# Identity and first low parts moved to VectorE, the passage between two stages prepared in the last channels, ScalarE issuing the first stacks, four mixing banks

## The chip, the cores and the metric

The kernel runs on one core of one Trainium2 chip. The core has five engines: TensorE (matmuls, into PSUM), VectorE, ScalarE, GpSimd, and SyncE, which here only issues DMAs; ScalarE and GpSimd can issue DMAs too. In the profile they are PE (PEld for TensorE's weight loads), DVE, ACT, POOL and SP. The metric is the device time of one execution, in microseconds.

## The reference

The input x has 128 samples, 64 channels and 1024 times, float32. Four steps follow one another, each adding to x:

```python
x = x + _L0_cond_ref(x, itok_B_8_3872, log_dt, C, log_A_real, A_imag, D)   # y = causal conv of (x*mask) along time
                                                                           #     with one kernel per channel, + D*x, * mask
x = x + _L1_cond_ref(x, itok_B_0_15, weights)       # einsum('bct,bcd->bdt', x, weights[condition]): 64x64 mixing of channels
x = x + _L2_cond_ref(x, itok_B_6_15, W2, bias, A2, B2)   # x @ W2.T + bias + (x @ A2[id].T) @ B2[id].T, rank 16
x = x + _L3_cond_ref(x, itok_B_0_2, W3, A3, B3)          # x @ W3.T + 0.5 * (x @ A3[id]) @ B3.T, rank 32
```

The mask is `arange(1024) < length` of each sample (step L0); the convolution kernel K of a channel is 2 Re sum_n Cs exp(dtA l) over 64 states. W2 and W3 are 1024 x 1024.

## The kernel before, in words

Products in float32 are replaced by three passes with two-part operands: each operand is split into a high part (a copy rounded to the type fp32r, made by ScalarE) and a low part (original minus high part, made by VectorE or GpSimd), and `PASSES` takes high x high, high x low and low x high.

**First block, preparation.** Since the L2 and L3 steps follow each other, their weights are merged into one matrix, (I + W2')(I + W3'). SP loads the eight 512 KB row blocks of W3 (`w3_raw`) and of W2 (`p2`). For each W3 block i an engine adds the identity to the block's diagonal part (`w3_identity`), ScalarE makes the high part `p3[:, i, 0]` and VectorE the low part (`p3_low`). The W2 blocks get an identity (`p2_identity`) and are staged in two buffers: `stage_high(n)` on ScalarE, `stage_low(n)` on GpSimd. TensorE runs 24 jobs in the order of the list `ORDER`, each into one of four PSUM targets of 1024 columns: d0, d4, the parameters of the convolution (`par`), the adapter products a3a and a3b, b2_0 to b2_2, c, row, b3, k0 and k1 (which build the convolution kernels from factors fac_u and fac_v), la0 to la3, d1, d5, d2, d6, d3, d7, b2_3. A job waits until the user before it of its target was read (`job_free`). d0 waits for `p3_lo` of each block in turn and for `staged_lo`. Meanwhile VectorE computes exponentials and the states' factors in a long chain of small operations on 64 x 64 elements, where every one waits for the one before (`link`): `exp_parts` first on `logs`, then on `decay`, up to `base_ready`; then the bias products, then the readers of the jobs. GpSimd makes the constants, the identities, the low parts and four large products of factors (128 x 2048), in this order: fac_v, fac_t, two times fac_u, fac_v, stage_low(4), fac_t.

**First block, convolution.** 64 channels, in groups of 8 (`UNROLL`), channel u of a group in buffer u % 4 for loads and u % 2 for the rest. Each channel's samples (`xt`) are multiplied with a Toeplitz table made from `lags`; 5.76 us of TensorE a channel. ScalarE makes high parts (`split_high`) for the next channel and copies the front half out (`front`), VectorE makes the low parts (`split_low`) and the back half (`back`). SP loads three channels ahead and stores each channel (`store_y`) to x1_d in HBM. After the last channel SP waits until its last stores have landed; this ends the block, and all engines go to the second block together.

**Second block.** 64 tiles of 128 rows (two samples of 64 channels) in 32 pairs. Each tile's x1 is loaded (`x1_in`), and for times past the sample's length `choose` puts the original x (`x_nat`) in its place: VectorE makes two 256-column pieces of a mask `late`, then a predicated copy of 512 columns. Four mixing quarters (`quarter`, 128 x 512 each, by the gathered mixing matrix `m_gath`) go through one PSUM bank, `MIX_BANK`; `take` on ScalarE copies each out, once as it is and, for three of them, as a high part. The pair's two tiles are multiplied with the merged 1024 x 1024 matrix by a scheme of seven products of quadrants (M1 to M7, Strassen-Winograd), with operands a11, s1, a12, a22, s2, s4, s3. The adapters' 96 columns (`h_table`, written by `h_high` and `h_low` from `tab2` and `tab3`, of which the second tile's is first made a `difference`) ride in M1, M5, M2 and M4; their results go through a small adapter product (`c_gath`, `hc`) into `hs`, and `low_rank` multiplies them with `stack`. In `pair(n)` of every engine's program the work of pair n+1 is prepared within pair n; only the first pair's preparation stands ahead of the loop, between the blocks. There, SP loads x1, x and the first tile's tables, ScalarE issues the second's, then SP loads `c_gath` and the stacks; GpSimd clears `m_gath` and fills `c_gath` before it gathers; VectorE chooses, sets fixed parts of `hrow`, `hc`, `hs` (twelve small instructions with `fix`), then makes the low parts.

Of the kernel before, what the change touches and what calls it, by code (L numbers as in the profile page):

```python
# [12 lines left out]
P = 128  # L13
# [30 lines left out]
def program(nc, x, xt_in, steps, cond, adapter, labeler, log_dt, ssm_c, log_a_real, a_imag, ssm_d,  # L44
# [143 lines left out]
    for i in range(1, 3):  # L188
        lags[i], o = at(f"lags{i}", [P, T], F32, o)
# [3 lines left out]
    b2_last, _ = at("b2_last", [P, 2, T], F32R, o)  # L193
# [21 lines left out]
    stack = both("stack", [P, 2, T], F32R)  # L215
    x1_in = both("x1_in", [P, T])
    x_nat = both("x_nat", [P, T])
    late = place("late", [P, HB], U16)
    tab2 = both("tab2", [P, 2, K8, R2])
    tab3 = both("tab3", [P, 2, K8, R3])  # L220
    m_gath, c_gath = both("m_gath", [P, P]), both("c_gath", [P, P])
    hrow, hc, hs = both("hrow", [P, P]), both("hc", [P, P]), both("hs", [P, 2, P], F32R)
# [55 lines left out]
    w3_ready, p2_ready = sem("w3_ready"), sem("p2_ready")  # L278
# [32 lines left out]
    b2_rows = b2_d.rearrange("a r h t -> (a r) h t")  # L311

    with nc.Block() as block:
        @block.sync
        def _(sp):
# [85 lines left out]
            for u in range(UNROLL):  # L401
                channel(GROUPS - 1, u, loads=False)
            for u in range(2):
                sp.wait_ge(x1_stored[u], count_in(GROUPS, 0, 2))
            sp.wait_ge(b2_stored, 16 * (AR // P))
# [3 lines left out]
            sp.wait_ge(a3_stored, 16)  # L409

        @block.gpsimd
        def _(pool):
# [43 lines left out]
            def w3_identity(i):  # L456
                pool.wait_ge(in_w3[i], 16)
                block_of = w3_raw[:, i, i * P:(i + 1) * P]
                tt(block_of, block_of, ident[:], ALU.add).then_inc(w3_ready, 1)

# [49 lines left out]
        def _(act):  # L510
# [12 lines left out]
            def stage_high(n):  # L523
# [4 lines left out]
                elif name[0] == "b":  # L528
                    act.wait_ge(in_b2, 16)
                else:  # L530
                    act.wait_ge(p2_ready, (1, 2, 0, 0, 0, 3, 4, 5, 6, 9, 10)[n])
# [26 lines left out]
            for i in range(K8):  # L558
# [4 lines left out]
                if i == K8 - 2:  # L563
                    act.wait_ge(trig_in, 1)
# [1078 lines left out]
```

## Time and profile before

| | us |
|---|---|
| median of 3 timed runs | 1518.61 (1517.77 to 1518.9) |
| the profiled execution | 1514.85 |
| its span, first to last instruction | 1512.9 |
| TensorE busy | 1458.1 (96%) |
| VectorE busy | 1118.1 (74%) |
| ScalarE busy | 630.9 (42%) |
| GpSimd busy | 134.9 (9%) |

A busy share is a mean over the stages: up to about 130 us the preparation runs, then the last preparation jobs and the convolution until 577.7 us, then the paired stage. "Idle before, <-X" at a row means that the engine stood for so long until X released it.

### The profile page before, as it was taken

The numbers are of one execution on the slowest core, as the hardware profiler recorded it, in microseconds if no ns is written. First come the engines' busy times: TensorE is split into PE (matmuls) and PEld (weight loads), VectorE is DVE, ScalarE is ACT, GpSimd is POOL, SyncE is SP. The second block draws the span as 40 slices with busy tenths as digits, with TensorE's granted clock in tenths as the row PEclk, the third lists the DMA queues.
The fourth block names the chain that finished last, engine by engine and source line by source line (L and its number), as shares of the span: only waits on it lengthen the run. The fifth ranks groups of instructions, "written<-read, shape, count | busy, mean of one in ns | idle before, by whom it ended". The sixth has DMA issues, their size and how long they took to land.

```text
span 1512.9 us, 33953 instructions
## 1 busy us (share of the span) xinstructions
PE 1458.1 (96%) x10624; PEld 1405.8 (93%) x10624; DVE 1118.1 (74%) x2320; ACT 630.9 (42%) x1249; POOL 134.9 (9%) x198
## 2 busy tenths in 40 slices
PE   6979999999999996999999999999999999999998
PEld 4867889999999995999999999999999999999998
DVE  7874478888888885677777777777777777777774
ACT  3330256566665652334334334334334334334332
POOL 6460210000000000000000000000000000000000
PEclk9989999999999996999999999999999999999999
DMA  8034068888888775445645645645655645645652
GB/s 303 17 134 114 11 205 286 276 274 270 275 275 271 276 248 182 160 147 162 193 146 162 193 146 162 193 146 160 195 146 159 195 146 158 197 146 156 198 146 78
DMA packets 121235, 276.15 MB, mean 183 GB/s; under 512 B 23881, under 2 KB 64333, under 8 KB 118545
## 3 DMA queue, kind: packets, MB, share of 16 engines
q1 hardware_dynamic: 110988, 241.67, 52.3%
q10 hardware_dynamic: 10214, 34.06, 5.6%
q8 instruction: 18, 0.29, 0.1%
q14 instruction: 15, 0.12, 0.0%
HBM read 200.72 MB, written 74.95 MB: 182 GB/s over the span
## 4 chain that ended last, share of the span: by engine, by line
PE 59%; DMA 1%; DVE 0%; issue 0%; ACT 0%; DVEq 0%; ACTq 0%; SPq 0%
PE ps L1537 23%; PE ps L1538 23%; PE ps L1508 8%; PE ps L1545 2%; PE ps L1547 2%; PE ps L1519 1%; DMA out<-y_out 1%; PE ps L1514 0%; DMA x_nat<-in_x 0%; ACT a L1282 0%; DVE weights L1399 0%; ACT xa L1284 0%; ACT weights L1294 0%; DVE x_in L1373 0%; DVE y_out L1486 0%
## 5 line engine op out<-in xcount | busy, mean ns | idle before, releaser
L1537 PE MATMUL ps<-weights,xs 128*128 128x256 f32 x1536 | 396.1, 289 | 0.0
L1538 PE MATMUL ps<-weights,xs 128*128 128x256 f32 (+1 forms) x1536 | 387.3, 291 | 0.0
L1537 PE MATMUL ps<-weights,xa 128*128 128x352 f32 (+1 forms) x1152 | 328.9, 314 | 4.6 <-DVE weights L1399 1.3
L1538 PE MATMUL ps<-weights,xa 128*128 128x256 f32 (+1 forms) x1152 | 322.8, 295 | 0.0
L1538 PEld LDWEIGHTS ps<-weights,xs 128*128 128x128 f32 x1536 | 292.3, 190 | 0.0
L1537 PEld LDWEIGHTS ps<-weights,xs 128*128 128x128 f32 x1536 | 291.3, 190 | 0.0
L1068 PE MATMUL ps<-toep,ut 128*128 128x512 f32 (+2 forms) x1152 | 228.2, 343 | 0.0
L1537 PEld LDWEIGHTS ps<-weights,xa 128*128 128x128 f32 x1152 | 216.9, 188 | 10.1 <-issue 10.1
L1538 PEld LDWEIGHTS ps<-weights,xa 128*128 128x128 f32 x1152 | 217.9, 189 | 0.0
L1068 PEld LDWEIGHTS ps<-toep,ut 128*128 128x128 f32 x1152 | 195.5, 190 | 16.8
L1282 ACT ACTIVATE a<-ps 128x512 f32<-128x512 f32 x128 | 76.7, 599 | 282.4 <-PE ps L1508 281.9
L1508 PE MATMUL ps<-m_gath,x_in 128*128 128x128 f32 x1024 | 139.1, 280 | 13.8 <-DVE x_in L1373 10.4
L1508 PEld LDWEIGHTS ps<-m_gath,x_in 128*128 128x128 f32 x1024 | 128.1, 196 | 14.8 <-DVE x_in L1373 12.2
L1256 POOL COPY m_gath<-mix 64x64 f32 x128 | 50.7, 396 | 826.1 <-PE ps L1508 713.7
L971 PE MATMUL ps<-p,staged 128*128 128x512 f32 x480 | 111.7, 394 | 12.6 <-POOL staged L454 10.4
L971 PEld LDWEIGHTS ps<-p,staged 128*128 128x128 f32 x480 | 91.2, 191 | 32.5 <-issue 10.8
L619 ACT ACTIVATE ut<-xt 128x896 fp32r<-128x896 f32 x64 | 61.0, 953 | 137.4 <-PE ps L1079 131.6
L1373 DVE COPY_PREDICATED x_in<-late,x_nat 128x512 f32<-128x512 uint16 x128 | 95.7, 747 | 19.5 <-DVE late L1368 19.5
L1079 PE MATMUL ps<-toep,ut 128*128 128x256 f32 x768 | 107.3, 289 | 0.0
L1079 PEld LDWEIGHTS ps<-toep,ut 128*128 128x128 f32 x768 | 95.8, 190 | 0.0
L903 DVE TENSOR_TENSOR ut<-xt,ut 128x896 fp32r<-128x896 f32 x64 | 69.9, 1093 | 16.7 <-ACT ut L619 16.7
L1294 ACT ACTIVATE weights<-tab 128x128 fp32r<-128x128 f32 (+1 forms) x256 | 71.3, 352 | 25.2 <-DVE tab L1390 25.2
(218 smaller groups left out, 2194.6 us busy)
## 6 DMA issues: line engine op xcount, KB each, us to landing
lags<-kern_d SPq DMA_DIRECT2D x64, 512.0 KB, 5.1
xt<-in_xt SPq DMA_DIRECT2D x64, 512.0 KB, 5.8
x_d<-yo SPq DMA_DIRECT2D x64, 512.0 KB, 2.9
x_in<-x_d SPq DMA_DIRECT2D x64, 512.0 KB, 5.9
x_nat<-in_x SPq DMA_DIRECT2D x64, 512.0 KB, 3.9
out<-y_out ACTq DMA_DIRECT2D x64, 512.0 KB, 5.5
stack<-b_d SPq DMA_DIRECT2D x130, 128.0 KB, 3.6
tab<-a_d SPq DMA_DIRECT2D x126, 128.0 KB, 2.1
```

The source lines that it names most:

```text
L619: copy(ut[u % 2][:, 0, 0:SPLIT], xt[u % BUFS][:, 0:SPLIT], ACT.Copy).then_inc(ut_hi, 1)
L903: tt(ut[u % 2][:, 1, 0:SPLIT], xt[u % BUFS][:, 0:SPLIT], f(ut[u % 2][:, 0, 0:SPLIT]), ALU.subtract).then_inc(ut_lo, 1)
L971: ins = mm(t[:, cols], staged[n % 2][:, a, c, :], p3[:, c, b, cols], start=c == a == b == 0, stop=c == K8 - 1 and a == 1)
L1068: mm(y[:, half * HB + i * P:(half + 1) * HB], xs[:, a, half * half_t + i, :], tp[:, b, 0:HB - i * P], start=i == a == b == 0, stop=False)
L1079: ins = mm(y[:, to:to + QT], xs[:, a, i, :], tp[:, b, at_col:at_col + QT], start=False, stop=i == half_t - 1 and a == 1)
L1256: ins = nc.gpsimd.tensor_copy(m_gath[v][rows, b * C:(b + 1) * C], mix[rows, bass.ds(s, 1), :].squeeze(1))
L1282: ins = copy(raw[:], mixing, ACT.Copy)
L1294: ins = copy(to, of, ACT.Copy)
L1373: nc.vector.copy_predicated(x1_in[v][:, cols], late[:], x_nat[v][:, cols]).then_inc(chosen[v], 1)
L1508: ins = mm(acc[:, MIX_BANK, i * P:(i + 1) * P], x1_in[v][:, c * P:(c + 1) * P], m_gath[v][:], start=True, stop=True)
L1537: mm(left[0], x_part, left[1], start=first and is_wide, stop=end, skip_group_check=True)
L1538: ins = mm(right[0], x_part, right[1], start=first and is_wide and H_AT[m] > 0, stop=end, skip_group_check=True)
```

## The change: what it does

- **Head.** The identity of W3's blocks and of p2[0], and the low part of the first staged block, move from GpSimd to VectorE, into a function `triangle` that runs within the first `exp_parts`, after the step with 1/720; the p3 low parts move in with them. ScalarE's two sine tables come after `stage_high(1)`. On GpSimd stage_low(4) moves ahead of the second fac_v product. A new semaphore `p2_first` counts p2[0].
- **Last channels.** SP loads the first pair's adapter tables after the loads of the last channels and the store of channel 60, and x of the first two tiles ahead of the store of channel 62; it issues the loads of x1 as soon as the stores have landed, still in the first block. ScalarE runs `h_high` of the first pair ahead of the last channel's `front`; VectorE runs `difference`, the masks of the first pair (eight, in `late_first`) and `h_low` around the last `back`. The SBUF tiles of the second block are placed so that these lie in buffers that are free by then.
- **Second block, first pair.** The quarters go into four banks without waiting for one another's reads; VectorE chooses in the order of the quarters, with no masks to make; its fixes come after `sums(0)`. GpSimd gathers before it fills `c_gath`. ScalarE issues the first stack loads; SP the rest.
- **Last pair.** VectorE makes y21 before y22, and the last tile's store is issued in two halves.

```diff
+            def triangle():
+                dve.wait_ge(consts, 2)
+                w3_identity(0)
+                dve.wait_ge(in_w2[0], 16)
+                tt(p2[0][:, 0, :], p2[0][:, 0, :], ident[:], ALU.add).then_inc(p2_first, 1)
+                p3_low(0)
+                w3_identity(1)
+                dve.wait_ge(staged_hi, 1)
+                tt(staged[0][:, 1], p2[0][:], f(staged[0][:, 0]), ALU.subtract).then_inc(staged_lo, 1)
+                for i in range(1, K8):
+                    if i + 1 < K8:
+                        w3_identity(i + 1)
+                    p3_low(i)
...
-            for i in range(K8):
-                w3_identity(i)
-                if i == 0:
-                    p2_identity(p2[0], 0, in_w2[0])
-                    stage_low(0)
             for i in BLOCKS[1:]:
                 p2_identity(p2[i], i, in_w2[i])
                 if i == 1:
+                    pool.wait_ge(staged_lo, 1)
                     stage_low(1)
...
+            stage_low(4)
             pool.wait_ge(fac_arg, 2)
             tt(fac_v[:], across(1), steps_of(1), ALU.mult).then_inc(fac_turns, 1)
-            stage_low(4)
...
# SP, end of the first block
-            for u in range(UNROLL):
+            for u in range(UNROLL - 3):
                 channel(GROUPS - 1, u, loads=False)
...
+            sp.wait_ge(toep_lo, C - 2)
+            sp.wait_ge(tri_ready, C - 2)
+            for v in range(2):
+                load_tables(sp, v, ids(sp, 0, v, B), ids(sp, 0, v, 2 * B))
+            channel(GROUPS - 1, UNROLL - 3, loads=False)
+            sp.wait_ge(toep_lo, C - 1)
+            sp.wait_ge(tri_ready, C - 1)
+            sp.wait_ge(conv_done, C - 3)
+            for v in range(2):
+                sp.dma_start(x_nat[v][:], x_rows[v]).then_inc(x_landed[v], 16)
+            channel(GROUPS - 1, UNROLL - 2, loads=False)
+            channel(GROUPS - 1, UNROLL - 1, loads=False)
+            for u in range(2):
+                sp.wait_ge(x1_stored[u], count_in(GROUPS, 0, 2))
+            for v in range(2):
+                sp.dma_start(x1_in[v][:], x1_rows[v]).then_inc(x1_landed[v], 16)
...
# ScalarE, last group of channels
             for u in range(UNROLL):
+                if u == UNROLL - 1:
+                    for v in range(2):
+                        h_high(act, 0, v)
                 channel(GROUPS - 1, u, ahead=u < UNROLL - 1)
...
# VectorE, last group of channels
-            for u in range(UNROLL):
+            for u in range(UNROLL - 1):
                 channel(GROUPS - 1, u, ahead=UNROLL - 1 - u)
+            difference(dve, 0)
+            dve.wait_ge(conv_done, C - 1)
+            for v in range(2):
+                for q in range(4):
+                    nc.vector.tensor_scalar(late_first[:, 2 * v + q // 2, q % 2 * QT:q % 2 * QT + QT], ramp[:], float(q * QT),
+                                            lens_cols[:, v:v + 1], ALU.add, ALU.is_ge).then_inc(masked, 1)
+            h_low(dve, 0, 0)
+            back(GROUPS - 1, UNROLL - 1)
+            h_low(dve, 0, 1)
...
# second block, ScalarE
-            load_tables(act, 1, ids(act, 0, 1, B), ids(act, 0, 1, 2 * B))
-            take(0, 0, a11, xa11)
-            take(0, 1, a21)
-            take(0, 2, a22, xa22)
-            h_high(0, 0)
+            for v in range(2):
+                load_stack(act, v, ids(act, 0, v, B))
+            take(0, 0, a11, xa11, FIRST_BANKS[0])
+            take(0, 1, a21, None, FIRST_BANKS[1])
+            take(0, 2, a22, xa22, FIRST_BANKS[2])
             s1_high(0)
-            h_high(0, 1)
-            take(0, 3, a12, xa12)
+            take(0, 3, a12, xa12, FIRST_BANKS[3])
...
# second block, TensorE
-            def quarter(n, q):
+            def quarter(n, q, bank=MIX_BANK):
...
-                ready(pe, quarter_read, 4 * n + q)
+                if bank == MIX_BANK:
+                    ready(pe, quarter_read, 4 * n + q)
...
+                if last_one:
+                    act.dma_start(out_rows[2 * n + 1, :, 0:HB], y_out[1][:, 0:HB]).then_inc(y_stored[1], 16)
+                    act.wait_ge(y22_added, n + 1)
+                    act.dma_start(out_rows[2 * n + 1, :, HB:T], y_out[1][:, HB:T]).then_inc(y_stored[1], 16)
```

`FIRST_BANKS = (MIX_BANK, SMALL_BANK, V_OWN, S_OWN)`; M1 writes to two others.

## Rows read from the trace of the kernel before

**Rows 1.** The page: span, and busy time (share of span) xinstructions by engine.

```profile
span 1512.9 us, 33953 instructions
PE 1458.1 (96%) x10624; PEld 1405.8 (93%) x10624; DVE 1118.1 (74%) x2320; ACT 630.9 (42%) x1249; POOL 134.9 (9%) x198
```

**Rows 2.** TensorE's waits: who waited for whom, us in total, times, longest.

```profile
PE ps L1059 <- DVE dt L909: 3.5, 2, 2.5
```

**Rows 3.** Timeline, 0 to 60 us: start, us, engine, line, operation, xcount, idle before.

```profile
8.69 0.49 POOL L463 TENSOR_TENSOR p<-p,ident 128x128 f32<-128x128 f32 x1 [0.92 <-DMA p<-in_L_cond_base_weight]
...
10.34 2.38 POOL L454 TENSOR_TENSOR staged<-p,staged 128x1024 fp32r<-128x1024 f32 x1 [1.17 <-ACT staged L534]
...
14.81 13.67 PE L980 MATMUL ps<-p,staged 128*128 128x512 f32 x48 [14.81 <-DVE p L668]
...
25.12 2.38 DVE L672 TENSOR_SCALAR e_k<-n 64x64 f32<-64x64 f32 x1
...
43.84 0.75 DVE L748 TENSOR_SCALAR b3t<-w_raw,bias_col 128x1024 f32<-128x1024 f32 x1
...
48.55 0.42 DVE L760 COPY part<-ps 128x256 f32<-128x256 f32 x1 [2.64 <-PE ps L995]
```

**Rows 4.** Tile w_raw, 0 to 30 us: xcount, ns min/median/max, first and last start.

```profile
L668 DVE TENSOR_TENSOR p<-w_raw,p x8: 1206/1226/1485, 13.6 to 24.0; 128x1024 fp32r<-128x1024 f32 x8
```

**Rows 5.** Timeline, 56 to 175 us, the jobs b2_0 to d1.

```profile
58.91 22.06 PE L971 MATMUL ps<-p,staged 128*128 128x512 f32 x96 [1.58 <-DVE raw L776]
...
86.82 4.39 POOL L454 TENSOR_TENSOR staged<-b2raw,staged 128x1024 fp32r<-128x1024 f32 x1
...
91.36 12.95 PE L971 MATMUL ps<-p,staged 128*128 128x512 f32 x48 [10.39 <-POOL staged L454]
...
115.31 0.66 DVE L845 COPY c_out<-ps 128x480 f32<-128x480 f32 x1 [4.47 <-PE ps L957]
...
127.53 47.69 PE L971 MATMUL ps<-p,staged 128*128 128x512 f32 x209 [0.61 <-DVE lora_out L869]
```

**Rows 6.** Timeline of SP's queue, 556 to 605 us.

```profile
561.33 17.59 SPq L371 DMA_DIRECT2D x_d<-yo  x4
581.66 0.34 SPq L1178 DMA_DIRECT2D x_in<-x_d  x1
...
583.00 0.43 SPq L1181 DMA_DIRECT2D x_nat<-in_x  x1
586.12 0.35 SPq L1167 DMA_DIRECT2D tab<-a_d  x1
```

**Rows 7.** Timeline, 556 to 605 us: ScalarE, VectorE and TensorE around the passage.

```profile
574.80 0.59 ACT L635 ACTIVATE yo<-ps 128x512 f32<-128x512 f32 x1
...
586.75 0.48 DVE L1368 TENSOR_SCALAR late<-ramp,lens_cols 128x256 uint16<-128x256 int16 x2 [8.24 <-DMA x_nat<-in_x]
...
588.17 2.08 PE L1508 MATMUL ps<-m_gath,x_in 128*128 128x128 f32 x8 [10.45 <-DVE x_in L1373]
...
592.60 0.17 DVE L1379 MEMSET hrow<- 128x128 f32 x1
...
594.95 0.69 DVE L1404 TENSOR_TENSOR xa<-a,xa 128x512 fp32r<-128x512 f32 x1
...
600.98 0.55 PE L1537 MATMUL ps<-weights,xa 128*128 128x256 f32 x1 [1.28 <-DVE weights L1399]
...
603.64 0.36 PE L1537 MATMUL ps<-weights,xa 128*128 128x256 f32 x1
```

**Rows 8.** The DMA view, issues by line: xcount, KB each, median us from issue to landing.

```profile
tab<-a_d SPq DMA_DIRECT2D x126, 128.0 KB, 2.1
...
tab<-a_d ACTq DMA_DIRECT2D x2, 128.0 KB, 5.0
```

**Rows 9.** The chain of waits, in order of time: a later quarter.

```profile
794.87 0.89 PE ps L1508 x8
```

**Rows 10.** Timeline, 1503 to 1513 us: the last issue.

```profile
1509.70 0.35 ACTq L1341 DMA_DIRECT2D out<-y_out  x1
```

More of the change, by code:

```diff
@@ new lines, in program, with over_pairs @@
+    PAIRS = TILES // 2
+    c_adapters = c_d[0:AR].rearrange("(a r) c -> a r c", r=R2)
+    x1_rows = x1_d.rearrange("(n b) c t -> n (b c) t", b=2)
+    x_rows = x.rearrange("(n b) c t -> n (b c) t", b=2)
+    out_rows = out.rearrange("(n b) c t -> n (b c) t", b=2)
+    H3 = slice(R2, R2 + R3)
+    def over_pairs(eng, body, end=PAIRS - 1):
+        body(0, False)
+        with eng.Fori(1, end) as n:
+            body(n, False)
+        for n in range(end, PAIRS):
+            body(n, n == PAIRS - 1)
@@ new lines, in halves, with load_stack @@
+    def halves(ap):
+        return ap.rearrange("p (k c) -> p k c", k=2)
+    first_rows = [sem(f"first_rows{v}") for v in range(2)]
+    masked = sem("masked")
+    def load_stack(eng, v, a):
+        for b in range(2):
+            row = b * (R2 + R3)
+            eng.dma_start(f(stack[v][row:row + R2]), b2_d[bass.ds(a[b], 1)].squeeze(0)).then_inc(stack_landed[v], 16)
+            eng.dma_start(f(stack[v][KS + row:KS + row + R2, 0]),
+                          b2_d[bass.ds(a[b], 1), :, 0, :].squeeze(0)).then_inc(stack_landed[v], 16)
@@ new lines, in h_high, with difference @@
+    def h_high(act, n, v):
+        act.wait_ge(tab_landed[v], 64 * n + 64)
+        if v == 1:
+            act.wait_ge(diffed, 2 * n + 2)
+        for m, part_of in products_of(v):
+            for to, of in zip(h_table(0, m), tables(v, part_of)):
+                ins = nc.scalar.activation(to, of, ACT.Copy)
+        ins.then_inc(h_hi[v], 1)
+    def difference(dve, n):
+        dve.wait_ge(tab_landed[1], 64 * n + 64)
+        for t in (tab2[1], tab3[1]):
+            nc.vector.tensor_tensor(t[:, :, K4:K8], t[:, :, K4:K8], t[:, :, 0:K4], ALU.subtract).then_inc(diffed, 1)
@@ L313, in program, with h_low @@
+    def h_low(dve, n, v):
+        dve.wait_ge(h_hi[v], n + 1)
+        if v == 1:
+            dve.wait_ge(diffed, 2 * n + 2)
+        for m, part_of in products_of(v):
+            for to, high, of in zip(h_table(1, m), h_table(0, m), tables(v, part_of)):
+                ins = nc.vector.tensor_tensor(to, of, f(high), ALU.subtract)
+        ins.then_inc(h_lo[v], 1)
     with nc.Block() as block:
@@ L679, in exp_parts @@
                     link(stt(q, q, 1.0 / n, r, ALU.add, ALU.mult))
+                    if n == 720 and between is not None:
+                        between()
                 link(ts(ki, k, 127.0, None, ALU.add))
@@ L694, in _ @@
             tt(frac[:], turns[:], tmp[:], ALU.subtract).then_inc(trig_in, 1)
-            for i in range(K8):
-                p3_low(i)
             exp_parts(decay[:], e_k[:, 0:N], e_f[:, 0:N], e_q[:, 0:N], e_2k[:, 0:N], e_i[:, 0:N])
@@ L1128, in program @@
-    PAIRS = TILES // 2
-    c_adapters = c_d[0:AR].rearrange("(a r) c -> a r c", r=R2)
-    x1_rows = x1_d.rearrange("(n b) c t -> n (b c) t", b=2)
-    x_rows = x.rearrange("(n b) c t -> n (b c) t", b=2)
-    out_rows = out.rearrange("(n b) c t -> n (b c) t", b=2)
-    H3 = slice(R2, R2 + R3)
-    def over_pairs(eng, body, end=PAIRS - 1):
-        body(0, False)
-        with eng.Fori(1, end) as n:
-            body(n, False)
-        for n in range(end, PAIRS):
-            body(n, n == PAIRS - 1)
@@ L1285, in take @@
                 ins.then_inc(quarter_read, 1)
-            def h_high(n, v):
-                act.wait_ge(tab_landed[v], 64 * n + 64)
-                if v == 1:
-                    act.wait_ge(diffed, 2 * n + 2)
-                for m, part_of in products_of(v):
-                    for to, of in zip(h_table(0, m), tables(v, part_of)):
-                        ins = copy(to, of, ACT.Copy)
-                ins.then_inc(h_hi[v], 1)
             def s1_high(n):
```

264 lines of the change are left out of this document (131 added, 133 removed).

## The prediction

> **What bounds the kernel now.** I read the busy line of the page first. TensorE is busy 1458.1 of the 1512.9 us span, so only some 55 us of TensorE's absence can be won anywhere [rows 1]. Next the list of TensorE's waits: behind three entries of over 10 us the next is 3.5 us [rows 2]. In all there are three large holes. One is the start: no matmul before 14.81 us, which waits for VectorE's low part of the first W block [rows 3]. One is inside the preparation: 10.4 us before the job b2_2 at 91.36, which waits for GpSimd's low part [rows 5]. One is the passage from the convolution to the paired stage: four mixing quarters of 2.05 us each spread from 588.17 to 600.98, after 10.45 us without a matmul, and then matmuls that stay long until 603.64: a record of L1537 is 0.55 us at 600.98 and 0.36 there, the first of the short ones [rows 7]. The paired stage itself (31 more pairs) has no hole worth naming. So the change can act in those three places and at the last store; the steady loops are the same code.
>
> **The start: identity and first low parts on VectorE.** After the change VectorE interrupts its exp chain after eight small operations, at about 7.5 us. p2[0] is on chip at 8.69 (GpSimd's add starts then) [rows 3], its identity is added by 9.0. One p3_low takes 1.21 us at best and 1.49 at worst [rows 4], so p3_low(0) ends at 10.2; the identity of block 1 (a 128x128 add; I take 0.3 us, GpSimd needs 0.49 for one [rows 3]) at 10.5; the low part of p2[0], same size as p3_low, at 11.8. GpSimd's version of that step took 2.38 us and began at 10.34 [rows 3]. The first matmul moves from 14.81 to about 11.8.
>
> That does not go to the end by itself, because VectorE's chain, not TensorE, sets when the next hole closes. Seven more rounds of 1.22 + 0.3 us, and 0.6 for meeting GpSimd, end the triangle near 23. Then GpSimd's second low part blocks VectorE: before, an operation of 0.2 us at 25.12 took 2.38 beside it [rows 3]. I let VectorE go on at 25.4. Fourteen small links of the interrupted chain are left, 0.28 us each (the pitch from 25.12 to 43.84, less its three stalls [rows 3]): 29.3, and 0.5 for GpSimd's remaining adds: 29.8. From there to the bias products the old chain took 43.84 - 25.12 = 18.7 us; 2.2 of stall and 0.8 of slowed links now lie ahead of it, so 15.7: the bias products begin at 45.5, 1.7 later than before. Two of them take 2.05; TensorE, early enough by then, has its transposed parameters at 46.0, so the copy that was at 48.55, behind a wait, comes at 47.6. The chain behind it (six bias products, the first lower_low) is 1.0 us earlier, and b2_0 starts near 57.9 instead of 58.91 [rows 3, 5]. Of the 3 us won at the first matmul, 2 turn into a wait for the parameters and before b2_0. Bounds: with every p3_low at 1.49 and each identity as slow as GpSimd's 0.49, b2_0 is 2 us later than that; if GpSimd's adds never meet it, 1 earlier.
>
> On that hangs one place where the Trainium skill speaks against the edit. The worst p3_low is 0.28 us above the best, and the small operation beside GpSimd's low part took 2.38 instead of 0.2 us [rows 3, 4]. The page "SBUF — State Buffer" (section "Who interferes with whom") says that a VectorE instruction with two SBUF inputs contends with a GpSimd instruction that reads SBUF, and whichever issues first holds the port for the whole instruction. By the rule the seven adds that GpSimd keeps would all hold up VectorE, 7 x 0.49 = 3.4 us instead of my 0.6, and the time would be 2.8 us above my forecast; by the row at most 8 x 0.28 = 2.2 us, 1.6 above it.
>
> **stage_low(4) ahead of the third factor product.** TensorE ends b2_1 at 58.91 + 22.06 = 80.97, now 79.9 [rows 5]. GpSimd ends its second fac_u product at 81.2 (where the next one began), now 80.1; the low part, which had stood behind a product of 5.7 us, starts at once and takes 4.39 as before (VectorE still holds it up; alone 2.38 [rows 3, 5]). b2_2 starts at 84.5 instead of 91.36. The factor product comes later by the same 4.4 us, but its reader on VectorE was not ready before about 89 anyway, and the two products together take what they took; the factors are 1 us earlier, as everything here. What is late next is VectorE again: from 104 us on it runs low parts, c, row, b3, the split constants, kern and lora copies one behind another until d1 may start at 127.53. Its idle time for TensorE in that chain was 4.47 us before the copy of c, and 0.35 after it [rows 5]. TensorE now brings c some 7 us earlier, so these 4.8 vanish, and no more; the store of the third b2 block then comes 0.3 us after VectorE wants it. So d1 starts 1.0 + 4.8 - 0.3 = 5.5 us earlier, and from there TensorE is continuous. Bounds of the whole head: 2.0 (VectorE's chain 3.5 later) and 7.5 (b2_0 a microsecond earlier still, and a low part of 2.38).
>
> **Work moved into the last channels.** SP issues the store of channel 60 at 561.33 [rows 6]. Behind it now come eight ids and eight table loads. Four ids cost it 2.7 us (from the end of its issue at 583.00 to 586.12), four table loads 1.9, so it is busy 9.2 us, until about 570.9, and the store of channel 61 is issued there instead of at 567.1. ScalarE needs that buffer again at 574.8 [rows 7]; the store lands 2.9 us after issue: 573.8, one us of cover. The x_nat loads follow, then the store of 62 on time. The last table lands 2.1 us after issue (the SP row; the ScalarE rows, behind 2 MB of loads, say 5.0) [rows 8], at 573.0. VectorE then does the differences (0.6), eight masks of 0.24 [rows 7] (1.9) and four lows (1.2): 576.8, under the end of the last channel at 577.7. ScalarE's highs end near 575. All of this is free, with 0.9 us of cover on VectorE. With a landing of 5.0 the last back part would be 2.2 late; that is the bound.
>
> **The passage.** The first instruction of the second block came at 581.66, when the last store had landed; x_nat[0], queued behind x1, was there at 586.75, 5.1 later [rows 6, 7]. Now x1 alone is loaded, issued by SP at 581.5 ahead of the block's end. A 512 KB load alone I put at 4.0 us, between the last store's 2.9 and that 5.1: landed 585.5. The masks are made, so one predicated copy (0.73) follows: first quarter at 586.4, 1.8 earlier than 588.17. GpSimd's gathers now come ahead of its c_gath work, the second done by 586.5, just in time. With four banks no quarter waits for ScalarE. Two quarters at the low clock (2.05 each) and two at the high one (0.89 each [rows 9]) end at 592.4, since b2_2 after its hole lost 12.95 - 22.06/2 = 1.9 us, so about 3.8 us pass at the low level of 1.2 GHz [rows 5]. ScalarE issues the stack loads first (four ids, eight DMAs at 0.5: to 589.2) and takes quarter 0 by 590.3; the low part is there at 591.1, and the tables are long split. So M1 starts at 592.4 instead of 600.98: 8.6. M1 runs at the high level at once: it had lost (603.64 - 600.98)/2 = 1.3. Together 9.9.
>
> Some is given back. M5 ends 6.5 us after M1 starts, at 598.9. M2 wants the copy of the first product out of PSUM, and ScalarE's queue has it behind s4's high part, which waits for VectorE's s4. VectorE now has its twelve fixes (592.60 to 594.95, 2.35 us [rows 7]) between the sums and the pair: sums end 594.7, fixes 597.1, s2, a12's low and s4 (0.65 each) 599.0, ScalarE's two copies of 0.6 [rows 7] 600.25. TensorE stands 1.35 us before M2. Net 8.5. Bounds 5 (x1 at 5.9, tables at 5.0) and 10.5 (no wait at M2, x1 at 3.3).
>
> **The last store.** Its issue is at 1509.70 and the span ends 3.2 us later [rows 10]. Halved, it moves 256 KB last instead of 512; at most 0.6, I take 0.2.
>
> **Sum.** 5.5 + 8.5 + 0.2 = 14.2 us. The profiled execution took 1514.85 us (span 1512.9 and 1.9 around it); it was 3.8 us faster than the median 1518.61 of the timed runs. I take the difference off the median: 1504.4.
>
> **Rivals.**
> A: VectorE in the head is blocked more than I allow, b2_0 starts later than before, the head brings 2. For it: the 2.38 for a 0.2 us operation. Against it: GpSimd has little to do until 17 us. 1507.9.
> B: SP's table block comes too late and the last back part waits 2.2 us. For it: 0.9 us of cover only. 1506.6.
> C: the clock stays at the low level through all four quarters and into M1 (before it did so through four spaced ones). 2.3 + 1.3 lost: 1508.0.
> D: no wait at M2, because x1 or ScalarE is quicker: 1503.
> E, the slower side: the low level lasts through pair 0 of the second stage, because short waits (M2's above all) keep breaking TensorE's work there. A pair is about 28 us of work at the high level, which would take twice that: 1504.4 + 28 + 1.3, about 1534. From 28 us of clock time at the low level on (14.2 us lost) the change is no gain. Against it: before, the clock rose 2.7 us into M1 and stayed [rows 7].
>
> **Chances.** Forecast 0.46, A 0.15, B 0.10, C 0.12, D 0.09, E 0.04, and 0.04 that A, B and C meet and leave nothing to be seen. A measurement here can tell about 0.2% (3 us) from no change: faster 0.92, same 0.04, slower 0.04. The range is 1499.5 to 1510.5: from both best bounds to A and C together.
>
> **What would show it.** First matmul near 11.8; a wait for the parameters near 45; b2_0 near 57.9 and b2_2 near 84.5; d1 near 122; the last channel's end with no new wait before its store; 8.7 us from the last convolution matmul to the first quarter; four quarters back to back in some 6 us, M1 6 us after the first quarter; a wait of 1 to 2 us before M2. I am wrong if b2_2 moves and d1 does not, if the last channel's back part waits for VectorE, or if M1 comes later than 595 (in the old times).

## The result, and the profile after

Median of 4 timed runs 1503.74 us (1502.53 to 1505.15), against 1518.19 (1517.1 to 1518.9, 4 runs) of the kernel before on the same chip: ratio 0.9908, 95% interval 0.9893 to 0.9922, 14.45 us less. The forecast was 1504.4. The profiled execution took 1502.63 us, its span is 1500.9 ([rows 1]: 1512.9).

The busy line of the page, to be read against [rows 1]:

```profile
PE 1456.2 (97%) x10624; PEld 1404.1 (94%) x10624; DVE 1114.5 (74%) x2330; ACT 631.1 (42%) x1249; POOL 117.3 (8%) x188
```

TensorE's matmuls are the same 10624. Its time without a matmul went from 54.8 to 44.7 us: that is 10.1 of the 12.0 us, and the other 1.9 are busy time. Its waits (who waited for whom, us in total, times, longest):

```profile
PE ps L1145 <- DVE staged L821: 11.8, 1, 11.8
PE ps L1573 <- DVE x_in L1455: 8.9, 1, 8.9
PE ps L1136 <- POOL staged L595: 4.8, 1, 4.8
PE ps L1225 <- DVE dt L1065: 4.6, 3, 2.4
PE ps L1209 <- DVE kern L1018: 2.8, 1, 2.8
...
PE ps L1602 <- ACT y_out L1386: 1.3, 2, 1.1
```

All three large holes are shorter, and the waits of the later quarters (2.5 and 0.8 before) are gone. The wait behind the copy of `kern` grew from 0.7 to 2.8 us, the one for `dt` in the convolution from 3.5 to 4.6. The last entry is new: it holds the wait before M2 (1.1).

**The head.** Timeline of all engines, 5 to 60 us (start, us, engine, line, operation, xcount, idle before), against [rows 3]:

```profile
10.26 0.29 DVE L806 TENSOR_TENSOR w_raw<-w_raw,ident 128x128 f32<-128x128 f32 x1
10.47 1.22 DVE L821 TENSOR_TENSOR staged<-p,staged 128x1024 fp32r<-128x1024 f32 x1
11.60 0.29 DVE L806 TENSOR_TENSOR w_raw<-w_raw,ident 128x128 f32<-128x128 f32 x1
11.83 13.97 PE L1145 MATMUL ps<-p,staged 128*128 128x512 f32 x48 [11.83 <-DVE staged L821]
...
18.49 2.62 DVE L810 TENSOR_TENSOR p<-w_raw,p 128x1024 fp32r<-128x1024 f32 x2
19.41 0.62 POOL L599 TENSOR_TENSOR p<-p,ident 128x128 f32<-128x128 f32 x1 [14.31 <-DMA p<-in_L_cond_base_weight]
...
20.61 0.82 POOL L599 TENSOR_TENSOR p<-p,ident 128x128 f32<-128x128 f32 x1 [0.58 <-DMA p<-in_L_cond_base_weight]
21.04 4.09 DVE L836 SCALAR_TENSOR_TENSOR e_q<-e_q,e_f 64x65 f32<-64x65 f32 x5
21.39 2.39 POOL L595 TENSOR_TENSOR staged<-p,staged 128x1024 fp32r<-128x1024 f32 x1
...
43.72 0.75 DVE L904 TENSOR_SCALAR b3t<-w_raw,bias_col 128x1024 f32<-128x1024 f32 x1
...
45.88 0.42 DVE L916 COPY part<-ps 128x256 f32<-128x256 f32 x1
```

The first matmul is 3.0 us earlier, and VectorE reaches the bias products at 43.72, as early as before (43.84). TensorE's timeline of the jobs b2_0, b2_2, the lora transposes and d1, against [rows 5]:

```profile
56.24 22.05 PE L1136 MATMUL ps<-p,staged 128*128 128x512 f32 x96 [1.57 <-DVE raw L932]
83.05 12.56 PE L1136 MATMUL ps<-p,staged 128*128 128x512 f32 x48 [4.76 <-POOL staged L595]
...
118.09 2.22 PE L1209 MATMUL ps<-ident,lora_a_raw 128*128 128x128 f32 x16 [2.76 <-DVE kern L1018]
120.91 19.33 PE L1136 MATMUL ps<-p,staged 128*128 128x512 f32 x84 [0.60 <-DVE lora_out L1025]
```

b2_0 is 2.7 us earlier, b2_2 8.3, d1 6.6. The 1.7 lost between are on VectorE's timeline, 92 to 122 us:

```profile
107.31 0.65 DVE L1001 COPY c_out<-ps 128x480 f32<-128x480 f32 x1
...
112.90 1.40 DVE L1011 CAST b_out<-b3t 1x1024 fp32r<-1x1024 f32 x2 [1.86 <-DMA b_d<-b_out]
...
116.82 2.34 DVE L1018 COPY kern<-ps 32x1024 f32<-32x1024 f32 x2
```

The wait of 4.47 before the copy of c is gone; the split constants wait 1.86 for the store that leaves their buffer free, and `kern`, queued behind them, is what TensorE waits for.

**The passage.** Timeline of SP's queue, VectorE and TensorE, 549 to 603 us, against [rows 6, 7]:

```profile
564.48 0.37 SPq L499 DMA_DIRECT2D x_d<-yo  x1
...
566.18 0.63 DVE L429 TENSOR_TENSOR tab<-tab 128x128 f32<-128x128 f32 x2 [0.28 <-DMA tab<-a_d]
...
570.90 0.42 DVE L1073 TENSOR_TENSOR yo<-ps,shared_in 128x256 f32<-128x256 f32 x1 [1.45 <-PE ps L1245]
575.36 0.82 SPq L550 DMA_DIRECT2D x_in<-x_d  x2
...
578.96 0.73 DVE L1455 COPY_PREDICATED x_in<-late_first,x_nat 128x512 f32<-128x512 uint16 x1 [6.23 <-DMA x_in<-x_d]
...
579.74 6.21 PE L1573 MATMUL ps<-m_gath,x_in 128*128 128x128 f32 x32 [8.88 <-DVE x_in L1455]
```

The last back part (570.90) waits for TensorE, not for the tables: all moved work is under cover. In the trace the store of the last channel lands 3.57 us after its issue at 571.73; in the trace before it was 2.61. In front of it SP has put 1 MB of x_nat, issued at 564.95, of which the second half lands at 572.76, and the store of channel 62, issued at 566.25, which lands at 574.08 (7.8 us later; 2.6 before). So the early x_nat loads are probably not free: the stores issued behind them land later than before, and x1 isn't loaded until the last store has landed. No run here has x_nat at another place, so this stays unproven. The wait before the first quarter is 8.88 instead of 10.45, and the 32 matmuls of the four quarters are one group without idle time. The same stretches of both kernels by engine (stretch, us, busy time and (x) of PE, PEld, DVE, ACT, POOL, then PEclk, DMA share, GB/s): hole, quarters, M1 and M5 until M2. Before:

```profile
577.72:588.17 10.45, 0.00 (x1) 0.00 (x1) 1.97 (x5) 0.00 (x0) 2.05 (x10) 0.60 0.62 236
588.17:600.98 12.81, 8.22 (x33) 7.16 (x33) 9.77 (x30) 6.24 (x16) 0.43 (x1) 0.50 0.71 172
600.98:608.92 7.94, 7.94 (x49) 7.94 (x49) 6.36 (x14) 2.42 (x5) 1.22 (x3) 0.82 0.94 312
```

After:

```profile
570.86:579.74 8.88, 0.00 (x1) 0.00 (x1) 2.56 (x7) 0.00 (x0) 0.98 (x5) 0.69 0.72 274
579.74:585.71 5.97, 5.97 (x32) 5.76 (x33) 2.64 (x4) 2.19 (x5) 1.05 (x6) 0.61 0.94 173
585.71:593.81 8.10, 6.96 (x51) 6.74 (x50) 6.92 (x19) 3.96 (x8) 0.94 (x4) 1.00 0.94 262
```

TensorE works through all of the quarters' stretch (5.97 of 5.97 us; before 8.22 of 12.81), and the granted clock is 1.00, the 2.4 GHz level, from M1 on; before it was still low there (0.82). From M1 to M2, though, 8.10 us pass with only 6.96 of work: M2 waits for ScalarE's copy (1.14). From the last convolution matmul to M2 it is 22.95 instead of 31.20 us: 8.25 less. With the 6.86 by which the convolution ends earlier, M2 comes 15.1 us earlier (608.92, 593.81).

At the end of the span only 12.0 are left. Between lie the pairs of the paired stage. From the start of M1 in the second pair to its start in the last, 30 pairs, it is 852.5 us in the profile before and 855.2 after: 2.8 given back before rounding. Before, 29 of the 30 are 28.4 us long. After, 11 are, and 16 are 28.53 or 28.54, without a longer wait of TensorE; these make some 2.1 of it, in code that the change doesn't touch. The rest lies in single longer pairs, the third above all (28.94). The last store is issued 3.3 us before the end of the span, against 3.2 [rows 10]: nothing from the halves.

### The profile page after: what moved, and what is told of

It is laid out like the page before. It is cut to its first block, busy times and chain, and to the rows that moved or that the text cites. A ratio compares the mean times of both kernels' runs of the same rounds, so it can differ in the third digit from the quotient of the medians.

```text
span 1500.9 us, 33974 instructions
## 1 busy us (share of the span) xinstructions
PE 1456.2 (97%) x10624; PEld 1404.1 (94%) x10624; DVE 1114.5 (74%) x2330; ACT 631.1 (42%) x1249; POOL 117.3 (8%) x188
## 4 chain that ended last, share of the span: by engine, by line
PE 87%; DVE 6%; DMA 3%; POOL 1%; issue 1%; ACT 1%; SPq 0%; DVEq 0%; ACTq 0%; POOLq 0%
PE ps L1602 23%; PE ps L1603 23%; PE ps L1234 13%; PE ps L1573 8%; PE ps L1245 6%; PE ps L1136 4%; PE ps L1225 3%; PE ps L1610 2%; PE ps L1612 2%; PE ps L1237 2%; DMA out<-y_out 1%; PE ps L1584 1%; DVE p L810 1%; DVE b3t L906 1%; DMA b_d<-b_last 1%
## 5 line engine op out<-in xcount | busy, mean ns | idle before, releaser
L1334 POOL COPY m_gath<-mix 64x64 f32 x128 | 46.1, 360 | 823.0 <-PE ps L1573 719.9
L1447 DVE COPY_PREDICATED x_in<-late,x_nat 128x512 f32<-128x512 uint16 x124 | 92.5, 746 | 18.9 <-DVE late L1442 18.9
L422 ACT ACTIVATE weights<-tab 128x128 fp32r<-128x128 f32 (+1 forms) x256 | 71.4, 353 | 26.6 <-DVE tab L429 26.5
```

Of the source, the lines that this page charges most:

```text
L422: ins = nc.scalar.activation(to, of, ACT.Copy)
L1334: ins = nc.gpsimd.tensor_copy(m_gath[v][rows, b * C:(b + 1) * C], mix[rows, bass.ds(s, 1), :].squeeze(1))
L1447: nc.vector.copy_predicated(x1_in[v][:, cols], late[:], x_nat[v][:, cols]).then_inc(chosen[v], 1)
```

## The experiments

Each ratio is against the kernel before, on the same chip. Where no ratio stands, the kernel ran once, and its time says little about a few us, since the runs of one kernel lie 1 to 6 us apart; such a run is read from its milestones. Milestones are from the profile of each. "Conv end" is the end of the last convolution matmul, q0 the first mixing quarter.

### The two halves of the change, each alone

Before, with the head's edits only:

```diff
+            def triangle(): ...            # identity, p3 low parts, stage_low(0) on VectorE
+            stage_low(4)                   # GpSimd, ahead of the second fac_v product
             tt(fac_v[:], across(1), steps_of(1), ALU.mult).then_inc(fac_turns, 1)
-            stage_low(4)
```

> The kernel before with the head's edits alone (triangle on VectorE, stage_low(4) ahead of the second fac_v product, sine tables later); second block and SBUF layout as before. Theory: the head is worth what the changed kernel's trace shows, d1 starting near 120.9 instead of 127.53, and passes on to the end unshortened: 6.6 us, a time near 1511.6, first convolution matmul 6.7 earlier, passage unchanged (10.4 us of wait, quarters spread over 12.8). Rival: the convolution's start waits for something else (its tables, the last low parts), and under 3 us arrive. On the paired stage: if its 28.53 us pairs in the changed kernel come from the new placement of the second block's tiles, all pairs are 28.40 here; if they are a matter of the run, some here are 28.5 too.

Measured: 1512.1 against 1519.41 us, ratio 0.9958 (0.9941 to 0.9974), 7.3 less. First matmul 11.9, b2_0 56.3, b2_2 83.1, d1 121.33; the passage is no shorter than before: q0 10.33 after conv end (10.45 before), M2 21.8 after q0 (20.8). The head's share of the gain is the head's edits alone.

The whole change without those:

```diff
-            def triangle(): ...
-            stage_low(4)                   # back behind the fac_v product, identities back on GpSimd
```

> The changed kernel with the head as it was before: the passage, the four banks, the layout and the last pair's edits alone. Theory: the passage is worth 8.4 us up to M2 of the first pair and the last store 0.2, independent of the head: near 1509.6 if the longer pairs are a matter of the run, near 1512.4 if the new placement causes them (then pairs of 28.5 us here). Sum of this gain and that of the head alone within 1.5 us of the changed kernel's. Rival: head and passage overlap in what they win (one shared limit), then the sum of the two single gains is over 17 us.

Measured: 1511.52 against 1519.41, ratio 0.9952 (0.9935 to 0.9968), 7.9 less. q0 8.46 after conv end, M1 6.1 after q0, M2 14.2 after q0 with a wait of 1.29. The halves don't need each other.

The changed kernel once more beside both:

> The changed kernel again, unedited. If the 28.53 us pairs come from its layout, most pairs have them again (25 to 60 percent at 28.39 were seen); if they are a matter of the run, the share changes widely, to none or to all. Time 1502.5 to 1505.2.

Measured: 1506.91 against 1519.41, ratio 0.9916 (0.9899 to 0.9932), 12.5 less, and outside the range expected; the halves' sum is 15.2. Each of the three differences is known to some 2.5 us, so 12.5 and 15.2 may well be the same. In these profiles 5 of 30 pairs are 28.53 us long with the head alone, 2 with the passage alone, and 27 with the whole change (857.5 us in all, 5.0 over the profile before). Of the 5.0, 27 times 0.13 are 3.5; another 1.3 is the third pair alone, of 29.66 us, in which TensorE waits 1.0 for ScalarE's copy out of PSUM. With the old passage (the kernel before, and the head alone) the second and third pairs are 28.40 to 28.53; with the new one, one of the two is 28.6 to 29.7 in every run. So a part of what the paired stage gives back follows the change; what holds ScalarE up there was not traced further.

Is it the code's layout that makes the pairs longer? The changed kernel a third time, on another chip:

> The changed kernel once more, on the same chip as the combined version, for the difference of the two and for the spread of three things between executions: landing of the last store (3.6 and 4.9 us seen), share of 28.53 us pairs, time at the low clock after the passage.

Measured: 1503.71 against 1517.14, ratio 0.9912 (0.9896 to 0.9929), 13.4 less; here 25 of the 30 pairs are 28.4 (853.9 us). Groups by line and shape, 610 to 1450 us (count, busy us, mean ns, idle before), first of the second run, then of this one:

```profile
L1603 PE MATMUL ps<-weights,xa 128*128 128x352 f32 x360 | 102.1, 325 | 0.0
L1603 PE MATMUL ps<-weights,xs 128*128 128x352 f32 x349 | 99.0, 326 | 0.0
```

```profile
L1603 PE MATMUL ps<-weights,xa 128*128 128x352 f32 x360 | 100.5, 320 | 0.0
L1603 PE MATMUL ps<-weights,xs 128*128 128x352 f32 x360 | 99.7, 317 | 0.0
```

The same program has both lengths, so layout alone doesn't decide it; the matmuls of 352 columns in M1 and M5 are longer, without a wait. What decides between them stays open.

### Four banks or one

```diff
-    FIRST_BANKS = (MIX_BANK, SMALL_BANK, V_OWN, S_OWN)
+    FIRST_BANKS = (MIX_BANK,) * 4
```

> The changed kernel with the four first quarters in one bank again, each waiting for the read of the one before. Theory: before, the quarters were 2.8 to 3.5 us apart; with the choices made early the pace is quarter plus ScalarE's copies (2.05 + 1.1 or 0.6, and s1's high part before the fourth), and the clock stays low: M1 starts about 6 us later than 585.7 (after the first quarter: 12 instead of 6), M1 at the low clock another 1.3; the wait of 1.1 before M2 disappears, since VectorE has the time. Net 5 to 6 us worse. Rival: the early tables and masks alone bring the quarters together and the banks are worth under 2 us.

Measured, one run: 1511.9 against 1519.41; the changed kernel on the same chip took 1506.91. TensorE's timeline:

```profile
581.57 2.07 PE L1573 MATMUL ps<-m_gath,x_in 128*128 128x128 f32 x8 [9.25 <-DVE x_in L1455]
585.86 2.04 PE L1573 MATMUL ps<-m_gath,x_in 128*128 128x128 f32 x8 [2.22 <-ACT xa L1364]
588.68 2.05 PE L1573 MATMUL ps<-m_gath,x_in 128*128 128x128 f32 x8 [0.78 <-ACT a L1362]
591.99 2.05 PE L1573 MATMUL ps<-m_gath,x_in 128*128 128x128 f32 x8 [1.27 <-ACT xa L1364]
```

All four quarters stay long and wait for ScalarE's reads between, and the stretch by engine of M1 and M5 has the clock at 0.77:

```profile
581.57:593.69 12.12, 7.86 (x32) 7.06 (x33) 4.35 (x7) 3.40 (x6) 0.99 (x5) 0.50 1.00 198
593.69:602.08 8.39, 8.39 (x50) 8.39 (x50) 7.57 (x21) 3.47 (x6) 1.69 (x4) 0.77 0.53 177
```

From q0 to M2 20.5 us against 14.1: the banks are worth 6.4 of the passage's 8.25, so the rival of under 2 us is out. One bank hides the wait at M2, since M1 comes later and longer.

### What M2 waits for

The twelve fixes of `hrow`, `hc` and `hs` put ahead of the choices, where VectorE waits for x1 anyway:

```diff
-            sums(0)
-            fix(nc.vector.memset(hrow[v][:], 0.0)) ...     # twelve
             for v, half in QUARTERS:
                 choose_first(v, half)
+            # the twelve fixes stand ahead of this loop
+            sums(0)
```

> The changed kernel with VectorE's twelve fixed-part instructions ahead of its first choice instead of behind the sums. VectorE was idle there for 6.2 us, 2.4 of them in the second block. Theory: the wait of 1.14 us before M2 came from the fixes; it goes, and M2 starts 8.1 minus 1.1 = 7.0 us after M1 (5.9 were two products: 2 x 3.3 = 6.7 without any wait); quarters not later than before by more than 0.3. Rival: M2's wait is ScalarE's own order (takes and high parts ahead of the copy), then at least 0.8 us of it stays.

Measured, one run: 1501.94 against 1521.67. M1 to M2:

```profile
588.11:594.77 6.66, 6.66 (x51) 6.66 (x50) 5.79 (x10) 4.27 (x8) 2.12 (x4) 1.00 0.87 242
```

6.66 instead of 8.10, no idle time: the fixes were M2's whole wait. The kernel's time tells less, since this profile had no pair of 28.53.

### stage_low(4) alone

```diff
-            stage_low(4)
             pool.wait_ge(fac_arg, 2)
             tt(fac_v[:], across(1), steps_of(1), ALU.mult).then_inc(fac_turns, 1)
+            stage_low(4)
```

> The changed kernel with stage_low(4) behind the second fac_v product again. Theory: b2_2 starts near 88.7 (83.05 + 5.7) instead of 83.05, the hole before it is 10.4 us again, and d1 starts about 4 to 5 us later than 121, since VectorE waits for TensorE's c again. Rival: VectorE's chain alone sets d1, and it starts within 1 us of 121.

Measured, one run: 1510.59 against 1521.67. TensorE's timeline:

```profile
88.97 13.80 PE L1136 MATMUL ps<-p,staged 128*128 128x512 f32 x48 [8.77 <-POOL staged L595]
...
125.99 4.37 PE L1136 MATMUL ps<-p,staged 128*128 128x512 f32 x18 [0.61 <-DVE lora_out L1025]
```

b2_2 is 5.9 us later, d1 5.1: of the 6.6 that the head brings at d1, moving one GpSimd instruction past another is 5.1, with the other edits in place, and all of those together the other 1.5. The move alone was not run.

### The wait for the store at the constants

The casts and low parts of the constants moved behind the lora copies on VectorE:

```diff
-            dve.wait_ge(b2_stored, 48)
-            ... tensor_copy(b2_out[rows, 0], b3t[rows]); tt(b2_out[rows, 1], ..., subtract)
             (kern copies, dcol, lora_out copies)
+            dve.wait_ge(b2_stored, 48)
+            ... tensor_copy(b2_out[rows, 0], b3t[rows]); tt(b2_out[rows, 1], ..., subtract)
```

> The changed kernel with VectorE's split of the constants (wait for the third b2 store, two casts, two subtractions: 112.90 to 116.79) moved behind the lora copies. Theory: VectorE's order sets d1; la2 waits no longer (2.8 us before) and d1 starts near 117.6 instead of 120.9, 3.3 us earlier, bound then by TensorE's own la3, and the convolution and the end move by the same 3.3. Rival: the constants' stores and the convolution kernels' store come later by 4 us and hold up what follows (weights of d2, or the first convolution): under 1 us arrives at the first convolution matmul.

Measured, one run: 1498.65 against 1521.67. TensorE's timeline:

```profile
113.30 3.71 PE L1209 MATMUL ps<-ident,lora_a_raw 128*128 128x128 f32 x32
116.77 8.44 PE L1136 MATMUL ps<-p,staged 128*128 128x512 f32 x36
```

No wait at the lora transposes, and d1 4.1 us earlier than after the change: the new wait was the constants' place in VectorE's queue.

### x1 in four loads

```diff
-                sp.dma_start(x1_in[v][:], x1_rows[v]).then_inc(x1_landed[v], 16)
+                sp.dma_start(x1_in[v][:, half * HB:(half + 1) * HB], ...).then_inc(half_landed[2 * v + half], 16)
```

> The changed kernel with the first x1 loads issued as four halves of 256 KB in the order of the quarters, each with its own semaphore. Theory: the first choice waits for 256 KB instead of 512, about 0.6 us earlier, and the second not 1.3 us behind it; first quarter 8.2 to 8.5 us after the last convolution matmul instead of 8.9 to 10.1. Rival: the landing is latency, and halved rows of 2 KB cost as much: first quarter not earlier, under 0.2 us.

Measured, one run: 1507.57 against 1521.67. VectorE's timeline and TensorE's:

```profile
580.75 2.89 DVE L1457 COPY_PREDICATED x_in<-late_first,x_nat 128x512 f32<-128x512 uint16 x4 [5.56 <-DMA x_in<-x_d]
```

```profile
583.16 6.44 PE L1575 MATMUL ps<-m_gath,x_in 128*128 128x128 f32 x32 [9.83 <-POOL m_gath L1336]
```

The first half is there 2.7 us after its issue (a whole load: 3.6), but SP ends the block two issues later, and TensorE now waits for GpSimd's gather, the second block's own: 9.83, where 8.2 to 8.5 were expected, and no gain. A second chain of nearly the same length stood beside the first.

### stage_low(0) on GpSimd

Only this step goes back, to see what VectorE and GpSimd cost each other.

```diff
-                tt(staged[0][:, 1], p2[0][:], f(staged[0][:, 0]), ALU.subtract).then_inc(staged_lo, 1)   # VectorE
+            stage_low(0)                                                                             # GpSimd
```

> The changed kernel with only the low part of the first staged block back on GpSimd (stage_low(0), 2.38 us there, 1.22 on VectorE); identities and W3 low parts stay on VectorE. Theory (GpSimd and VectorE block each other while both read SBUF): GpSimd takes over when p3_low(0) or the identity of block 1 ends, near 10.5, VectorE's p3_low(1) waits until about 12.8; first matmul near 12.9 instead of 11.8, and the last W3 low part near 22, 1 us later than 21.1; b2_0 later by 1. Rival (they run beside each other at little loss, as the 1.49 against 1.21 us of the kernel before suggests): first matmul near 12.6, but p3_low(1) is done by 12.0 and VectorE's chain comes 1.2 us earlier than in the changed kernel, since it has the low part no longer.

Measured, one run: 1506.43 against 1517.14. Timeline, 8 to 26 us:

```profile
10.01 0.29 DVE L806 TENSOR_TENSOR w_raw<-w_raw,ident 128x128 f32<-128x128 f32 x1
10.20 2.35 POOL L595 TENSOR_TENSOR staged<-p,staged 128x1024 fp32r<-128x1024 f32 x1 [5.10 <-ACT staged L668]
...
11.20 1.49 DVE L806 TENSOR_TENSOR w_raw<-w_raw,ident 128x128 f32<-128x128 f32 x1 [0.91 <-DMA w_raw<-in_L_cond_W]
...
12.69 13.20 PE L1143 MATMUL ps<-p,staged 128*128 128x512 f32 x48 [12.69 <-POOL staged L595]
```

The identity that starts within GpSimd's low part takes 1.49 instead of 0.29 us and ends 0.14 after it. As the theory had it, the next low part starts at 12.62 only, and the last ends at 21.93 against 21.12 in the first profile of the changed kernel. The first matmul is at 12.69 (11.54 to 11.85 in the three profiles of the changed kernel), b2_0 at 56.6 (56.0 to 56.2), where 1 us was expected. At d1 nothing can be told: 121.39, and the three have 120.91 to 121.39.

### What the runs point to, in one kernel

The constants late; the fixes inside pair 0; gathers in the first block; the first stacks issued by SP; and the last channel stored and loaded in halves, the front halves by ScalarE:

```diff
+            act.dma_start(x1_d[:, C - 1, 0:HB], yo[1][:, 0:HB]).then_inc(last_stored[0], 16)
+            act.wait_ge(last_stored[0], 32)
+            act.dma_start(x1_in[v][:, 0:HB], x1_rows[v][:, 0:HB]).then_inc(half_landed[2 * v], 16)
```

> A version made of what the runs point to: constants' split behind the lora copies; the last channel stored in two halves (ScalarE issues the front half as soon as it is copied out, and then the front halves of x1 of the first two tiles; SP the back halves); GpSimd's gathers in the first block; VectorE's twelve fixed parts within the first pair, behind s3's low part; the first stacks issued by SP behind the loads of x1 for pair 1 instead of by ScalarE ahead of its takes. Expected against the changed kernel: d1 4.1 us earlier; first quarter 6.5 to 7 us after the last convolution matmul instead of 8.9 to 10; M1 2 us earlier relative to it, no wait before M2 (1.1). Sum 7.5, a time 1496 to 1499 where the changed kernel has 1503.7 to 1506.9. Rival: the passage is bound by the end of the first block (the landing of the last store, then 0.5 to 1 us), so that the front halves wait anyway and only the 5.2 of constants and M2 arrive. A new risk: stacks that land too late for the first low-rank product, about 17 us after M1; each us counts fully.

Measured: 1498.44 against 1517.14, ratio 0.9875 (0.9859 to 0.9892), 18.7 less, and 5.3 less than the changed kernel on the same chip (1503.71). That the single run with late constants alone took 1498.65 shows how little more is in the rest. d1 118.07; q0 8.4 after conv end, where 6.5 to 7 were expected (8.9 to 10.1 in the changed kernel's three profiles); M1 to M2 6.65. What came is the constants (2.8 at d1) and the fixes (1.4 at M2), as the rival had it. But the fixes now stand in VectorE's queue ahead of the adapter's copy, and TensorE waits for that:

```profile
PE ps L1588 <- DVE hrow L1493: 1.3, 1, 1.3
```

So most of the 1.4 is lost again within the first pair; with the fixes ahead of the choices this wait was 0.2. The halves brought little or nothing: the front store is issued at 566.54, but x1's first loads at 573.23, 6.7 us later. In the trace the transfers land one behind another: x_nat at 569.99 and 571.18, the store of channel 62 at 572.89, the front store at 573.13, the back store at 573.77. The passage is bound by the landing of stores, and after them of x1.

The profile of this kernel has 26 pairs of 28.53 and took 1502.4; its three other runs took 1497.53 to 1498.67. The pairs are the likely reason, since 26 of them are 3.4 us, but the other runs have no trace.

## Why the prediction was right, step by step

- **Start.** First matmul 11.8, measured 11.83. The bias products were put at 45.5 and came at 43.72, and this term is the one mis-sized, by the length of a round above all. I summed a round as 1.22 + 0.3; the records of both overlap, and a round is 1.34 (10.26 to 11.60). So the triangle ended at 21.1 and not at 23.0, and GpSimd's 2.4 us fell on the chain's first links instead of ahead of them. By 25.13 five of the fourteen links were done; nine of 0.28 and the 15.7 of the old chain give 43.4, 0.3 short of what was measured. Contention with GpSimd's adds was near its estimate: I had 0.6 within the triangle and 0.5 after it. Only two of the seven adds began within the triangle (19.41 and 20.61; they took 0.62 and 0.82 us instead of 0.46), and they cost VectorE 0.19 on its last low part (1.41 instead of 1.22) and 0.26 on the first link (0.48 instead of 0.22). The other five slowed a link each, to 0.38 to 0.42 us from about 0.2. That is 1.4 in all.
- **The wait for the parameters**, foreseen near 45, did not come: TensorE runs from one job into the next up to 54.7, VectorE has its bias products done at 45.8 and copies the parameters at once (45.88; before, it waited 2.64 there and copied at 48.55, [rows 3]). So TensorE's 3 us arrive almost whole at b2_0: 56.24, 2.7 earlier, and not 57.9, 1.0 earlier.
- **The rule of the Trainium skill** on that page ("SBUF — State Buffer", "Who interferes with whom") is borne out where a VectorE add with two SBUF inputs started within a GpSimd low part: 1.49 against 0.29 us in the run with stage_low(0) on GpSimd. The price that I had drawn from it, seven times the whole length of an add, 3.4 us, did not come; all seven adds met a VectorE instruction, and each cost it some 0.2 us, 1.4 in all. What counts is how much of the one instruction is left when the other starts, and that is read from start times.
- **b2_2** from b2_0: 26.6 predicted, 26.8 measured. With stage_low(4) back it is 32.5 (56.51 to 88.97), so this move did it.
- **d1.** 5.5 predicted, 6.6 measured, by two errors of opposite sign: the chain was 3.4 earlier (109.61 to 106.17 at its last b2 low part) instead of 1.0, and the wait for the third store was 1.86 instead of 0.3. The 4.8 of idle time went as predicted. The prediction named the right next limit, VectorE's order, but not how cheaply it could be lifted.
- **Last channels.** Store of channel 61 predicted at the end of the table block, 570.9 in the old times and so 564.3 with d1's 6.6; measured 564.48. The differences begin at 566.18 (566.4). Rival B did not happen.
- **Passage.** q0 8.88 after conv end (8.7): the loads of x1 took 3.6 instead of 4.0 and the last store landed later, at 4.5 after conv end instead of 3.8, behind the x_nat loads. Quarters 5.97 (6), M1 14.85 after conv end instead of 23.26, 8.4 against 8.6. The granted clock was 1.00 from M1 on, and rival C did not happen in this run. The window 575.99 to 583.77 of the constants' experiment shows how near it is, with 0.50 through all four quarters (M1 and M5 behind them: 0.96):

```profile
575.99:583.77 7.78, 7.21 (x33) 6.92 (x33) 2.86 (x5) 2.77 (x5) 1.02 (x6) 0.50 1.02 159
```

- **M2.** Wait 1.35 predicted, 1.14 measured, and its cause shown. Rivals D and E did not happen.
- **Tail.** 0.2 predicted, nothing measured.
- **The sum.** 6.86 + 8.25 = 15.1 at M2 against 14.0 predicted to that point; the paired stage gave 2.8 back in the profile, a cost that no term foresaw and that the prediction put at nothing. The profiles are 12.2 us apart and the medians 14.45, within 0.3 of the forecast. The profile before was 3.3 us quicker than its median and the one after 1.1. It would be explained if the timed runs of the kernel before had the longer pairs more often than its profile does, but no trace here shows that. So part of the agreement is chance: in the two later sets of runs the changed kernel was 12.5 and 13.4 us under the kernel before. Three slips in the prediction's arithmetic changed nothing here: A and C together give 1511.5, not 1510.5; both best bounds give about 1500, not 1499.5; and A, B and C together would leave 4.9 us of the gain, which is more than the 3 us that it says can be told from no change.

## What to carry to other kernels

When a hole is closed, read the next engine's queue in its order: here a split of constants that nobody waited for stood ahead of a copy that TensorE waited for, and moving it was worth 3 to 4 us more. Between two stages, prepare the next one's tables, masks and high parts in the last steps of the old one, give the first steps a PSUM bank each, and put constant fills where the engine waits for a transfer: ahead of the choices they cost nothing, within the first pair they held up the adapter. Once the work was out of the way, the passage through HBM cost the landing of the last store and then of the first load; what was queued ahead of that store probably lengthened it, and splitting brought nothing in either form tried. Before a difference of 1 to 4 us is read from one run's time, look whether the steady loop ran at the same pace.

## What was not expected of the hardware

- A pair of the paired stage takes 28.40 or 28.53 us, in the same program and at a granted clock of 1.00. The matmuls of 352 columns in M1 and M5 take 317 to 320 or 325 to 326 ns on average. Both paces occur within one execution, and the share changes from one run to another (from none to 27 of 30 pairs long). Over 30 pairs this is up to 3.5 us, more than several edits here are worth.
- The last 512 KB store of the convolution landed 3.6 us after its issue in one run and 4.8 in another of the same kernel, which moves the whole second half. In the kernel before it was 2.6.
- After a hole of 8.9 to 10.1 us the quarters' mean granted clock was 0.61 in one run of the changed kernel, 0.66 and 0.55 in two others, and 0.50 in the kernel with late constants: the stretch at the 1.2 GHz level was not equally long each time. M1 came 5.65 to 7.8 us after the first quarter, for that reason and for short waits in between (up to 0.6 us).
- A small VectorE instruction that started within a GpSimd low part lasted until about its end: 1.49 us instead of 0.29 in the run with stage_low(0) on GpSimd, and 2.32 instead of 0.22 for a link of the chain in the profile after. In the run with stage_low(0) on GpSimd two GpSimd adds beside VectorE's low parts took 1.83 and 1.44 us instead of 0.46.
